# Attention inside the second stage with 16 whole-height products in place of 64 small ones, operands spread by DMA

## The reference

```
h = _layernorm(x, axis=-1) * (1 + cb) + sb
qkv = h @ Wqkv.T + bqkv          # 4 heads of 32 channels
scores = einsum('bhqd,bhkd->bhqk', q, k) / sqrt(32)
att = softmax(scores, axis=-1)
o = einsum('bhqk,bhkd->bhqd', att, v)
y = _layer_norm(h + o @ Wo.T + bo, g1, be1)
z = _layer_norm(y + _moe(y, Wg, W1, b1, W2, b2), g2, be2)   # 8 experts, the best one for each row
x = x + gb * z
```

## Time and profile before

| | |
|---|---|
| runs | 1226.2, 1226.77, 1223.17 us (median 1226.2) |
| span of the profiled execution | 1223.0 us |
| TensorE busy | 1102.8 us, 90% |
| VectorE busy | 971.2 us, 79% |
| ScalarE busy | 921.4 us, 75% |
| GpSimd busy | 854.5 us, 70% |
| second stage | about 803 to 1047 us |

### The profile page before, as it was taken

The page is one execution under the profiler, slowest core; times in us unless marked ns, Lnnn a source line. Parts: engine busy times, 40 slices in busy tenths (PEclk is TensorE's granted clock), DMA queues, the critical chain, the costliest instruction groups (busy, mean ns, idle before and its releaser), DMA issues. The chain is left out here.

```text
span 1223.0 us, 49591 instructions
## 1 busy us (share of the span) xinstructions
PE 1102.8 (90%) x17489; PEld 902.1 (74%) x17489; DVE 971.2 (79%) x4190; ACT 921.4 (75%) x3404; POOL 854.5 (70%) x685
## 2 busy tenths in 40 slices
PE   4899999999999999999999999947999984599992
PEld 2688888888888888888888887725787773488882
DVE  6898998898898898988989987546788764188884
ACT  2689989989889899899899898836776752366661
POOL 2777877877877878777878776554576677067775
PEclk9899999999999999999999999969988885699996
DMA  6766666766666666667667667352243123676110
GB/s 197 208 166 167 177 169 164 182 166 168 175 167 170 177 167 170 176 156 183 166 170 175 163 156 188 96 184 80 62 137 103 55 81 135 172 196 178 58 37 22
DMA packets 111026, 180.88 MB, mean 148 GB/s; under 512 B 19726, under 2 KB 64177, under 8 KB 110656
## 3 DMA queue, kind: packets, MB, share of 16 engines
q1 hardware_dynamic: 102944, 158.53, 50.3%
q0 software_dynamic: 6400, 16.82, 3.8%
q10 hardware_dynamic: 1440, 2.36, 0.8%
HBM read 35.20 MB, written 24.73 MB: 49 GB/s over the span
## 5 line engine op out<-in xcount | busy, mean ns | idle before, releaser
L612 POOL TENSOR_TENSOR qk<-mm,sw 128x1024 f32<-128x1024 f32 x128 | 305.0, 2383 | 96.2 <-DMA sw<-mm 96.1
L685 ACT ACTIVATE pr<-sm,mn 128x96 f32<-128x96 f32 x1024 | 368.6, 371 | 0.0
L618 POOL TENSOR_TENSOR pr<-pr,ri 128x768 f32<-128x768 f32 x128 | 189.1, 1478 | 73.0 <-DVE ri L540 72.9
L501 DVE TENSOR_TENSOR mm<-bank,cos 128x512 f32<-128x512 f32 x256 | 175.3, 685 | 69.9 <-PE bank L324 58.8
L685 ACT ACTIVATION_READ_ACCUMULATOR pr<-sm,mn 128x1 f32 x1024 | 202.2, 197 | 0.0
L513 DVE CUSTOM_DVE_ANT_0 sm<-bank,msk 128x96 f32<-128x96 f32 x1024 | 190.9, 252 | 3.4 <-PE bank L350 3.4
L502 DVE TENSOR_TENSOR mm<-bank,sin 128x512 f32<-128x512 f32 x256 | 174.0, 680 | 0.0
L377 PE MATMUL bank<-pT,vw 96*64 96x64 f32 x4096 | 147.5, 225 | 0.0
L377 PEld LDWEIGHTS bank<-pT,vw 96*64 96x64 f32 x4096 | 129.8, 138 | 17.1 <-issue 5.8
L676 ACT ACTIVATE pT<-bank 96x512 f32<-96x512 f32 x256 | 137.4, 588 | 0.5 <-PE bank L392 0.5
L392 PE MATMUL bank<-ident,pr 128*96 128x128 f32 x1024 | 133.6, 274 | 0.0
(11 more groups left out here) (206 smaller groups left out, 2492.8 us busy)
## 6 DMA issues: line engine op xcount, KB each, us to landing
sw<-mm SPq DMA_DIRECT2D x512, 128.0 KB, 2.4
vw<-vn SPq DMA_DIRECT2D x128, 192.0 KB, 2.6
vw<-vn SPq DMA_DIRECT2D x128, 128.0 KB, 2.3
rr<-sorted_scratch SPq DMA_DIRECT2D x72, 192.5 KB, 2.8
vw<-vn SPq DMA_DIRECT2D x96, 64.0 KB, 2.2
xt<-in_x SPq DMA_DIRECT2D x16, 256.0 KB, 3.9
x_scratch<-x SPq DMA_DIRECT2D x16, 256.0 KB, 2.5
rr<-x_scratch SPq DMA_DIRECT2D x16, 256.0 KB, 3.1
```

Source lines behind the costliest of these rows:

```text
L501: dve.tensor_tensor(mm[s % 2][:, 0, j, :], PJ[u % 2][:, :], cos[:, :], ALU.mult)
L612: pool.tensor_tensor(qk[i % 2][:, :, 32:], mm[i % 2][:, 0, :, :], sw[i % 2][:, :, :], ALU.add)\
L618: pool.tensor_tensor(t, t, ri[i % 2][:, :].unsqueeze(2).to_broadcast([P, 8, WK]), ALU.mult)\
L685: ins = act.activation(pr[i % 2][:, h, p, :], ms_[i % 2][:, h, p, :], ACT.Exp, scale=-1.0, bias=mn[i % 2][:, h, p:p + 1], accum_out=sums[i ...
```

## The change

Scores. After the projection of the keys is evacuated to `kT`, SyncE copies each head's 32 partitions to a large tile `kx`, which is zero elsewhere: head h's keys stand on partitions 32h to 32h+31 in column block h. A product over all 128 partitions of `qT` (32 columns stationary) with 4 x 32 columns of `kx` then gives the scores of all four heads at once. 16 such products replace 64, and all heads land in one bank, `S[u % 2]`, so that one product writes the mask, one reduction takes the maximum and one subtraction follows.

Values. After the transposed probabilities are in `pT`, SyncE copies each 32-partition strip j to its own block of `px`, zero elsewhere. 16 products of 32 stationary value columns with 4 x 32 columns of `px` replace 64. They are placed after the scores, one slot later than before (`s - 3` instead of `s - 2`), and write one bank `O[u % 2]`, which ScalarE evacuates with one instruction at the head of its slot.

Waits. The scores wait for `kx` instead of `kT`, the values for `px` instead of `pT`. `kx` and `px` have one buffer each: the copies wait for the scores or values of the quad before. The copies of slot s are eight DMAs on SyncE, four for `kx` of quad s and then four for `px` of quad s-2, written ahead of the row load of quad s+4 in SyncE's program. ScalarE clears `kx` and `px` once, at the start. Three semaphores are merged with others.

```diff
+            def spread(u):
+                if quad(u):
+                    sp.wait_ge(s_ke, u + 1)
+                    if u == 0:
+                        sp.wait_ge(s_ao, 3)
+                    else:
+                        sp.wait_ge(s_sc, u)
+                    for h in range(4):
+                        r = slice(32 * h, 32 * h + 32)
+                        sp.dma_start(kx[r, h, :], kT[u % 2][r, :]).then_inc(s_kx, 16)
+                if quad(u - 2):
+                    sp.wait_ge(s_pe, u - 1)
+                    if u >= 3:
+                        sp.wait_ge(s_pv, u - 2)
+                    for j in range(4):
+                        r = slice(32 * j, 32 * j + 32)
+                        sp.dma_start(px[r, j, :], pT[u % 2][r, :]).then_inc(s_px, 16)
+
             for u in range(NQ):
+                if u >= 4:
+                    spread(u - 4)
...
+            for u in range(NQ - 4, NQ + 2):
+                spread(u)
...
                 u = s - 1
                 if quad(u):
+                    if u >= 2:
+                        pe.wait_ge(s_dd, u - 1)
+                    pe.matmul(S[u % 2][:, :], identb[:, :], blk_m[:, :, :], start=True, stop=False, skip_group_check=True)
                     pe.wait_ge(s_qe, u + 1)
-                    pe.wait_ge(s_ke, u + 1)
-                    if u >= 2:
-                        pe.wait_ge(s_oe, 4 * (u - 1))
-                    for h in range(4):
-                        pe.matmul(X[h][:, 0:P], identb[:, :], blk_m[:, :, :], start=True, stop=False, skip_group_check=True)
+                    pe.wait_ge(s_kx, 64 * u + 64)
+                    sc = S[u % 2][:, :].rearrange("p (h j k) -> p h j k", h=4, j=4)
                     for j in range(4):
                         for g in range(4):
                             c = slice(g * P + 32 * j, g * P + 32 * j + 32)
-                            for h in range(4):
-                                r = slice(32 * h, 32 * h + 32)
-                                ins = pe.matmul(X[h][32 * g:32 * g + 32, 32 * j:32 * j + 32], qT[u % 2][r, c], kT[u % 2][r, c],
-                                                start=False, stop=True, skip_group_check=True)
+                            ins = pe.matmul(sc[32 * g:32 * g + 32, :, j, :], qT[u % 2][:, c], kx[:, :, c],
+                                            start=False, stop=True, skip_group_check=True)
                     ins.then_inc(s_sc, 1)
+                u = s - 3
+                if quad(u):
+                    pe.wait_ge(s_px, 64 * u + 64)
+                    pe.wait_ge(s_ve, u + 1)
+                    if u >= 2:
+                        pe.wait_ge(s_oe, u - 1)
+                    ob = O[u % 2][:, :].rearrange("p (j g q) -> p j g q", j=4, g=4)
+                    for g in range(4):
+                        for h in range(4):
+                            d = slice(32 * h, 32 * h + 32)
+                            ins = pe.matmul(ob[d, :, g, :], va[u % 3][:, g, d], px[:, :, h * P + 32 * g:h * P + 32 * g + 32],
+                                            start=True, stop=True, skip_group_check=True)
+                    ins.then_inc(s_pv, 1)
...
             act.wait_ge(s_eo, 1)
...
+            for t in (kx, px):
+                act.activation(t[:, :, :].rearrange("p a (b c) -> p (a b) c", c=P),
+                               ident[:, :].unsqueeze(1).to_broadcast([P, 16, P]), ACT.Copy, scale=0.0).then_inc(s_ao, 1)
             for s in range(FIRST, LAST):
...
+                u = s - 3
+                if quad(u):
+                    act.wait_ge(s_pv, u + 1)
+                    if u >= 2:
+                        act.wait_ge(s_r, r_use[("wo", u - 2)] + 1)
+                    act.activation(oT[u % 2][:, :], O[u % 2][:, :], ACT.Identity, bias=fb[:, 2:3]).then_inc(s_oe, 1)
...
-                    for h in range(4):
-                        dve.tensor_reduce(mx[:, 4 * h:4 * h + 4], X[h][:, 0:P].rearrange("p (j k) -> p j k", j=4),
-                                          AX.X, ALU.max).then_inc(s_mx, 1)
+                    sc = S[u % 2][:, :].rearrange("p (r k) -> p r k", k=32)
+                    dve.tensor_reduce(mx[:, :], sc, AX.X, ALU.max).then_inc(s_mx, 1)
...
+                    dve.tensor_tensor(dd[:, :, :].rearrange("p h (j k) -> p (h j) k", j=4), sc,
+                                      mx[:, :].unsqueeze(2).to_broadcast([P, 16, 32]), ALU.subtract).then_inc(s_dd, 1)
```

More of the change, by code:

```diff
@@ L754, in phase2 @@
     oT = [sbt(p2, f"foT{n}", [P, 4 * P]) for n in range(2)]
+    kx = sbt(p2, "fkx", [P, 4, 4 * P])
+    px = sbt(p2, "fpx", [P, 4, 4 * P])
     uu = [sbt(p2, f"uu{n}", [P, 4, C]) for n in range(2)]
@@ L807, in phase2 @@
     s_sl = sem("s_sl")
-    X, RING = banks[0:4], banks[4:8]
+    s_kx = sem("s_kx")
+    s_px = sem("s_px")
+    S, O, RING = banks[0:2], banks[2:4], banks[4:8]
     FIRST, LAST = -3, NQ + 6
@@ L935, in _ @@
             pool.memset(xnh[:, :], -0.5).then_inc(s_rx, 1)
-            pool.memset(pad[:, :], 0.0).then_inc(s_pz, 1)
-            pool.wait_ge(s_pz, 1)
-            pool.memset(pad[:, IX:IX + 1].bitcast(I32), OOB).then_inc(s_pz, 1)
+            pool.memset(pad[:, :], 0.0).then_inc(s_pw, 1)
+            pool.wait_ge(s_pw, NG + 1)
+            pool.memset(pad[:, IX:IX + 1].bitcast(I32), OOB).then_inc(s_pw, 1)
             pool.wait_ge(s_l2, 16 * 6)
@@ L1085, in _ @@
                     ins.then_inc(s_r, 1)
-                u = s - 2
-                if quad(u):
-                    pe.wait_ge(s_pe, u + 1)
-                    pe.wait_ge(s_ve, u + 1)
-                    if quad(u + 1):
-                        pe.wait_ge(s_dd, 4 * (u + 1) + 4)
-                    for g in range(4):
-                        for h in range(4):
-                            for j in range(4):
-                                r = slice(32 * j, 32 * j + 32)
-                                ins = pe.matmul(X[j][32 * h:32 * h + 32, 32 * g:32 * g + 32],
-                                                va[u % 3][r, g, 32 * h:32 * h + 32],
-                                                pT[u % 2][r, h * P + 32 * g:h * P + 32 * g + 32],
-                                                start=True, stop=True, skip_group_check=True)
-                    ins.then_inc(s_pv, 1)
                 u = s - 5
@@ L1204, in _ @@
                 if quad(u):
-                    act.wait_ge(s_dd, 4 * u + 4)
+                    act.wait_ge(s_dd, u + 1)
                     if u >= 2:
@@ L1211, in _ @@
                     act.wait_ge(s_r, r_use[("k", u)] + 1)
+                    if u >= 2:
+                        act.wait_ge(s_kx, 64 * (u - 1))
                     act.activation(kT[u % 2][:, :], ring("k", u)[:, :], ACT.Identity, bias=fb[:, 1:2]).then_inc(s_ke, 1)
@@ L1241, in _ @@
                     ins.then_inc(s_cn, 1)
-                u = s - 2
-                if quad(u):
-                    act.wait_ge(s_pv, u + 1)
-                    if u >= 2:
-                        act.wait_ge(s_r, r_use[("wo", u - 2)] + 1)
-                    for j in range(4):
-                        act.activation(oT[u % 2][:, j * P:(j + 1) * P], X[j][:, 0:P], ACT.Identity, bias=fb[:, 2:3])\
-                            .then_inc(s_oe, 1)
                 e = s - 5
@@ L1255, in _ @@
                         .then_inc(s_whi, 1)
-            act.wait_ge(s_pz, 2)
+            act.wait_ge(s_pw, NG + 2)
             act.wait_ge(s_pad, 1)
@@ L1323, in _ @@
                     dve.wait_ge(s_sc, u + 1)
-                    for h in range(4):
-                        dve.tensor_reduce(mx[:, 4 * h:4 * h + 4], X[h][:, 0:P].rearrange("p (j k) -> p j k", j=4),
-                                          AX.X, ALU.max).then_inc(s_mx, 1)
+                    sc = S[u % 2][:, :].rearrange("p (r k) -> p r k", k=32)
+                    dve.tensor_reduce(mx[:, :], sc, AX.X, ALU.max).then_inc(s_mx, 1)
                     if u >= 1:
                         dve.wait_ge(s_ex, u)
-                    for h in range(4):
-                        dve.wait_ge(s_mx, 4 * u + h + 1)
-                        dve.tensor_tensor(dd[:, h, :].rearrange("p (j k) -> p j k", j=4),
-                                          X[h][:, 0:P].rearrange("p (j k) -> p j k", j=4),
-                                          mx[:, 4 * h:4 * h + 4].unsqueeze(2).to_broadcast([P, 4, 32]),
-                                          ALU.subtract).then_inc(s_dd, 1)
+                    dve.wait_ge(s_mx, 2 * u + 1)
+                    dve.tensor_tensor(dd[:, :, :].rearrange("p h (j k) -> p (h j) k", j=4), sc,
+                                      mx[:, :].unsqueeze(2).to_broadcast([P, 16, 32]), ALU.subtract).then_inc(s_dd, 1)
                 u = s + 1
@@ L1350, in _ @@
                     dve.tensor_reduce(sums[:, :], pp[u % 2][:, :, :].rearrange("p h (j k) -> p (h j) k", j=4), AX.X, ALU.add)\
[L1351 to L1352 removed]
+                        .then_inc(s_mx, 1)
+                    dve.wait_ge(s_mx, 2 * u + 2)
                     if u >= 2:
```

26 lines of the change are left out of this document (11 added, 15 removed).

## The result

The changed kernel takes 1247.8 us (median of 4 runs, 1243.9 to 1251.1), the kernel before 1225.3 on the same chip (4 runs, 1223.2 to 1226.8): 1.0185 times as long, 95% interval 1.0158 to 1.0211. The forecast was 1230 with a range of 1214 to 1246. Slower was right, the size was not: some 22 us instead of 4, and 1.8 us beyond the end of the range.

A forecast was written before the change was run, and what follows sets the result against it. The ring of eight SyncE copies, not TensorE's work, was taken to set the slot: with the start and half clock, quad 15's q,k came 8.6 us later, less 4.7 at the end, +3.9: 1230 us, range 1214 to 1246.

The forecast's parts named there:

- The fifth rival: TensorE's issue gaps, 10 us, don't come from instruction fetching and stay: +3 us; counted within the forecast's spread.
- TensorE's work: Scores and values groups on TensorE take 1.0 us each; by TensorE alone a slot would be 10.3 us.
- The third rival: Column groups don't overlap, so scores and values take 4.4 us each: in full +64 us, 1290; chance 0.07.
- Landing: The last of SyncE's eight copies in a slot lands 2.4 us after its issue; issue and landing together 7.2 us.
- the ring: q,k to kT 3.05 us, eight SyncE copies landing 0.05 + 7.2, values 1.0 before the next q,k: 11.3 us a slot.
- The end: GpSimd's closed scatter chain opens 14.8 us behind quad 15's q,k instead of 19.5, giving 4.7 us back.
- The start: In the first slots, q,k of quad 3 starts at 845.8 against 836.33: 9.5 us lost.
- The clock: TensorE's clock falls to half in two slots out of three, adding 0.55 us a slot; full slots 11.9 us.
- Tight ring: Eight copies land in 6.8 to 7.0 us, clock stays up, slots 10.9 to 11.2 us: -8.3 us, 1218; chance 0.22.
- copies hidden: Copies land before TensorE arrives, so the slot is TensorE's or GpSimd's, 10.3 us: 1207; chance 0.08.
- The fourth: Half clock in every slot, or copy issues at 0.81 us: 13.0 us a slot, +16 us, 1242; chance 0.16.
- The point of decision: From 12.4 us a slot on, it decides against the change; twelve slots had taken 12.1 and the end returns 4.7.

The follow-up runs named there:

- e_shift_half: Changed kernel with 64 tiny TensorE products, half a 16 KB block of instructions, ahead of the first slot: 1237.3 us, 1.0120 of the kernel before.
- e_busy: Changed kernel with three wide products in front of each of TensorE's waits for px and yT: 1236.8 us, 1.0081 of the kernel before.
- e_shift_full: Changed kernel with 128 tiny TensorE products, a whole block of instructions, ahead of the first slot: 1243.8 us, 1.0154 of the kernel before.
- e_scatter_after: Changed kernel, GpSimd issuing a slot's four scatters only after that slot's px copies have landed: 1244.5 us, 1.0153 of the kernel before.
- e_scatter_hold: Changed kernel, GpSimd issuing the scatters of quads 5 to 15 only behind all slots: 1277.1 us, 1.0405 of the kernel before.
- e_values_late: Changed kernel with the values group moved behind the transposed probabilities and oT evacuated after yT: 1224.4 us, 1.0007 of the kernel before.
- e_late_w2: e_values_late with the 2 MB load of W2 (and b2) issued three quads earlier: 1217.8 us, 0.9946 of the kernel before.
- e_nokx: Changed kernel without the four kx copies in each slot, px copies kept: 1213.7 us, 0.9921 of the kernel before.
- e_fill: e_late_w2 with the values one place later, between t3 and the logits, and a fourth buffer for v: 1204.1 us, 0.9852 of the kernel before.

## Why the prediction was wrong in size and right in sign

**What bounds the kernel.** Right. With 15 blocks of instructions for 39 the issue gaps fell from 10 us to 1.8, as they should if they were the instruction stream; no run changes the blocks alone. The fifth rival, gaps that stay, is out. One count in the text is double: 96 small products go, not 192, and the trace has 196 matmuls less a slot (126 for 322). Nothing in the sum uses it.

**TensorE's work.** Right: 32 instructions in 1.08 us (forecast 1.0), for the scores and for the values. The third rival, by which a weight load would wait for products of the same rows, is out: four column groups overlap. Without copies TensorE's slot is 10.5 us (forecast 10.3).

**Issue of the copies.** Right: median 590 ns, 2.45 us for four, so 0.63 each and not the 0.81 of the upper bound.

**Landing.** This is the term of the ring that was mis-sized: 2.4 us from the earlier trace rows, 3.6 to 4.3 measured in the slots of quads 7 to 15. The row was right for a copy that meets nothing (2.1 in the slot of quad 2, 2.3 to 2.4 in e_shift_half and e_busy). The prediction had read that 39 blocks are fetched in the stage and used it for TensorE alone; it did not ask which engines carry them. The change takes away most blocks and then lines the remaining one up with the copies. Eight slots from quad 5 to 13 took 102.3 us instead of 95.2, the two to quad 15 26.9 instead of 23.4: +10.6 of the 21.7 us missed. Of these, 2.4 us are in the slots of quads 5 and 6, where the copies landed in 2.1 and 2.4 us and half clock alone made the scores late; about 8 are in slots with a late landing. With the fetch elsewhere, e_shift_half, the eight took 93.5 and the two 21.6, even under the forecast, but in a fast execution; between the medians of e_shift_half and e_shift_full lie 6.5 us, between their profiled executions 15.7.

**The end.** 19.0 instead of 14.8, +4.2. Same cause in large part: 15.3 in e_shift_half, 18.6 in e_shift_full. The landing was 3.9 us there for 2.3 in e_shift_half, and the copies were issued 0.95 us later, since `q`,`k` ran at half clock.

**The start.** +6.9 us. Of these 2.3 were there before the first slot (`q`,`k` of quad 0 starts at 817.40, in the kernel before at 815.14; in the profiles of the other kernels here it lies between 813.9 and 819.6, so one execution does not show it as an effect of the change). +3.0 came up to quad 3: the slots of quads 0 to 2 took 10.4, 10.4 and 12.9 us for 9.8, 9.6 and 11.3. `kT` is done at +4.5 there, not at +3.05, since `q`,`k` run at half clock. The text of the prediction had expected that for quads 2 to 4, its sum counted quad 2 at full clock, and for quads 0 and 1 it was hardly counted. Part of this is chance: with the same code up to there e_busy, e_scatter_after and e_scatter_hold took 30.1 to 30.3 us for these three slots, under the forecast of 30.7, where the changed kernel took 33.7. +1.6 came from quads 3 and 4, with the wait of 5.6 us for `kx` behind the W2 load. "Under a microsecond" was wrong for that slot: the load takes 9.3 us to land and the copies stood behind it. Moving it took 2.5 us off that slot in the closed ring, and 6.6 us off the whole once the ring was open (e_values_late against e_late_w2).

**The clock.** It falls in most full slots, about as forecast. In those of 12.1 and 12.2 us (quads 8 and 10) it costs next to nothing, since the scores at half clock end when the copies have just landed (complete at +11.12 and +11.00, values at +11.16 and +11.09); in those of 13.5 to 14.6 (quads 6, 11, 12, 14) values or `q`,`k` or late scores run at it and the ring grows. The forecast had 0.55 us a slot. That it can come down with no wait but that for `yT`, e_nokx showed (13.72 against 10.47 us); in e_fill, with the values in that place, it stayed up. e_busy did not show it: filling the waits with products left the middle slots long.

**The rivals.** Tight ring, copies hidden, no overlap: out. The fourth, half clock or slow issues at 13 us a slot, 1242, is what came nearest in time; it was reached by a late landing and half clock in some slots, not by slow issues: from quad 3 to 15 a slot took 156.45 / 12 = 13.0 us. The point of decision that the prediction gives for it, 12.4 us a slot, is wrong by its own terms, since it leaves out the 9.5 us lost at the start; with them it is (981.37 + 4.7 - 845.8) / 12 = 11.7, which the forecast itself was over.

The three missed terms are 6.9 + 10.6 + 4.2 = 21.7 us, which is 25.6 - 3.9. So the step that failed is the landing of the `px` copies, taken at 2.4 us in every slot; it accounts for about 8 us of the middle and a good part of the 4.2 at the end. Half clock and the start are the rest, and they differ by some microseconds from one execution to the next.

## What to carry to other kernels

A cheaper product that needs its operand moved by DMA is worth what its place in the order allows: put the consumer where another engine's latency has to be covered anyway, and not between the step that starts the copies' producer and the step itself. With the same copies the kernel was 22 us slower than the one before on a closed ring and 19 us faster in e_fill. When a loop body is about one block of instructions long, look where in the loop the fetch falls, because it stays there; a landing time from a quiet stretch is a lower bound.

## What the runs showed of the hardware

- The fetch of one 16 KB block of TensorE's instructions delays the completion of copies in flight by 1.2 to 1.6 us, although it moves little (2.04 us after the last issue without it and 3.3 with it while scatters were held back, 2.3 to 2.5 and 3.6 to 4.3 beside scatters): all but one or two of the 64 increments of the semaphore come in time. Half a block more of instructions ahead of the loop moves the values from +11.2 to +9.7, a whole block brings them back to +11.4.
- 32 instructions of 128 rows and 32 columns with 128 moving, f32, in four column groups: 1.08 us, at half clock 1.94.
- The clock can fall to half for 6.9 us in each of several slots in a row with a wait of only 0.92 us in each (13.72 for 10.47 us), and with the same wait it can stay up (e_nokx, slots of quads 8 to 10 and 11 to 14).
- Four scatters (512 rows together) in flight at the same time cost such copies 0.3 us without a block of instructions in flight (2.3 to 2.5 us against 2.04 with the scatters held back) and about 0.6 with one (median 3.9 against 3.3).
